# Moving two state products and an add between VectorE, GpSimd and TensorE in a fused scan and expert kernel

## The reference

```python
xn = layernorm(x)                                  # x: 32 sequences x 512 steps x 256 channels
# state space part, 16 states n per channel
delta, B, C = split(xn @ W_deltaBC.T, [64, 80])
delta  = softplus(delta @ W_dt.T + b_dt)
deltaA = exp(delta[..., None] * -exp(A_log))
BX     = delta[..., None] * B[:, :, None, :] * xn[..., None]
hs     = scan over the 512 steps: h[t] = deltaA[t] * h[t-1] + BX[t]
y      = einsum('blds,bls->bld', hs, C) + D * xn
# 8 experts, each takes its 128 best rows of every sequence
G, I = top_k(softmax(xn @ Wg), 128)
ffn  = scatter_add(G * (gelu(xn[I] @ W1 + b1) @ W2 + b2), I)
out  = x + y + ffn
```

## Time and profile before

| | |
|---|---|
| median of 3 runs | 2426.65 us (2425.75 to 2430.33) |
| the profiled execution | 2422.32 us, its span 2420.4 us |
| busy share of the span | PE 94%, PEld 75%, DVE 97%, ACT 86%, POOL 89% |
| DVE instructions with C | L1008 x448, mean 1216 ns |
| POOL adds to ysum | L585 x415 and 32 first ones |
| loads of b_wide | x128, 512 KB each, median 4.5 us to landing |

### The profile page before, as it was taken

One profiled execution on the slowest core, in us unless ns is written; L12 is line 12 of the kernel. 1 busy time (PEld: TensorE's weight loads), 2 busy tenths in 40 slices (PEclk: granted clock), 3 DMA queues, 4 the chain that ended last, 5 costly groups with the idle time before them and its releaser, 6 DMA issues. The chain is left out here.

```text
span 2420.4 us, 33772 instructions
## 1 busy us (share of the span) xinstructions
PE 2286.8 (94%) x10756; PEld 1816.4 (75%) x10756; DVE 2349.7 (97%) x1975; ACT 2074.3 (86%) x3629; POOL 2146.5 (89%) x1235
## 2 busy tenths in 40 slices
PE   7749999999999999999999999999999999999996
PEld 4437777777777777777777777777778777777775
DVE  5799999999999999999999999999999999999997
ACT  7748889898888888988888889888898989888884
POOL 5527999999999899999999999999999999999997
PEclk9969999999999999999999999999999999999998
DMA  9967575645656565555656555565646456565444
GB/s 344 338 209 266 158 221 157 177 136 148 168 147 173 145 161 141 165 154 134 184 137 173 136 166 145 141 176 143 177 127 180 127 151 163 149 173 139 128 127 79
DMA packets 151649, 403.04 MB, mean 167 GB/s; under 512 B 19536, under 2 KB 88240, under 8 KB 134832
## 3 DMA queue, kind: packets, MB, share of 16 engines
q1 hardware_dynamic: 84208, 316.72, 38.2%
q0 software_dynamic: 66048, 83.92, 20.6%
q10 hardware_dynamic: 1216, 0.23, 0.0%
HBM read 323.72 MB, written 91.75 MB: 172 GB/s over the span
## 5 line engine op out<-in xcount | busy, mean ns | idle before, releaser
L585 POOL TENSOR_TENSOR ysum<-ysum,prod 128x1024 f32<-128x1024 f32 x415 | 1121.4, 2702 | 20.3 <-DVE prod L1008 12.1
L997 DVE TENSOR_TENSOR_SCAN bank_x<-decay,bank_x 128x1024 f32<-128x1024 f32 x448 | 1024.7, 2287 | 8.9 <-DVE bank_x L936 0.5
L1163 PE MATMUL bank_l<-ext,w_sb 128*128 128x256 f32 x4096 | 968.9, 384 | 28.2 <-ACT og L757 22.6
L1229 PE MATMUL bank_l<-w_sb,hid 128*128 128x256 f32 x4096 | 939.0, 382 | 0.0
L1163 PEld LDWEIGHTS bank_l<-ext,w_sb 128*128 128x128 f32 x4096 | 760.3, 191 | 166.5 <-ACT og L757 31.0
L1229 PEld LDWEIGHTS bank_l<-w_sb,hid 128*128 128x128 f32 x4096 | 767.5, 190 | 130.0 <-issue 29.0
L717 ACT ACTIVATE decay<-delta,a_sb 128x511 f32<-128x511 f32 x1024 | 641.9, 707 | 15.8 <-POOL delta L517 14.6
L936 DVE TENSOR_TENSOR bank_x<-du,bank_b 128x1024 f32<-128x1024 f32 x512 | 617.6, 1206 | 4.7 <-ACT bank_b L748 3.2
L726 ACT ACTIVATE hid<-bank_l,b_all 128x256 f32<-128x256 f32 x1024 | 431.5, 475 | 203.8 <-PE bank_l L1163 200.7
L1008 DVE TENSOR_TENSOR prod<-bank_x,c_all 128x1024 f32<-128x1024 f32 x448 | 544.9, 1216 | 0.1
L540 POOL DMA_INDIRECT out<-og,idx_all x256 | 410.0, 1601 | 43.8 <-POOL ysum L585 42.5
(11 more groups left out here) (117 smaller groups left out, 1958.9 us busy)
## 6 DMA issues: line engine op xcount, KB each, us to landing
c_all<-bc_rows SPq DMA_DIRECT2D x128, 1024.0 KB, 5.1
b_wide<-bc_rows SPq DMA_DIRECT2D x128, 512.0 KB, 4.5
w_sb<-in_w SPq DMA_DIRECT2D x32, 1024.0 KB, 9.3
decay<-in_x SPq DMA_DIRECT2D x32, 512.0 KB, 6.8
xn_rows<-c_all SPq DMA_DIRECT2D x32, 512.0 KB, 6.5
out<-yrow POOLq DMA_DIRECT2D x32, 512.0 KB, 8.5
xr<-xn_rows SPq DMA_DIRECT2D x30, 512.0 KB, 6.0
bc_rows<-prod SPq DMA_DIRECT2D x32, 192.0 KB, 5.1
```

The source lines that it names most:

```text
L585: nc.gpsimd.tensor_tensor(ysum[:, m % 2], first, prod[:, i], ALU.add).then_inc(sum_done, 1)
L997: nc.vector.tensor_tensor_scan(into, decay[:, k % 2, i].rearrange("p c t -> p (c t)"), bank_x[:, s % 2], 0.0, ALU.mult, ALU.add).then_inc( ...
L1163: i = nc.tensor.matmul(bank_l[(q + v) % 2][:, (f % 2) * UT:(f % 2 + 1) * UT], w1_sb[:, e2, hc, f * P:(f + 1) * P], ext[:, v % 2, hc], star ...
L1229: i = nc.tensor.matmul(o, hid[:, w % 2, f, c * K:(c + 1) * K], w2_sb[:, w_par, f], start=False, stop=(f == FC - 1 and c == UB - 1))
```

## The change

States 4, 14 and 15 are now `GP_STEPS`, so POOL makes three products per batch; `KEPT` is (14, 15). The scans of 14 and 15 write to `kept[:, 0]` and `kept[:, 1]`, POOL multiplies in place, and both stay terms of their own, which PE sums. State 8 is now an ordinary state. Of the last batch DVE makes the products 14 and 15 itself. The two gathers of a unit stand behind step 0 and behind step 3 of the quarter. In the first quarter ACT copies the B rows 2 and 3 and PE spreads 0 and 1. The last y is summed term by term, as each term gets ready, into `bank_t` and `bank_l[0]`.

```diff
-GP_STEPS = (4, 8)
-KEPT = 8
+GP_STEPS = (4, 14, 15)
+KEPT = (14, 15)
-WIDE = (1, 2)
+WIDE = ((2, 3), (1, 2), (1, 2), (1, 2))
...
+        def by_gp(s):
+            return s % N in GP_STEPS and not (s // N == NB - 1 and s % N in KEPT)
+        def stays(s):
+            return s % N in KEPT and s // N < NB - 1
...
 # SP, load_b_wide(u)
-                held(b_ready, (u - 1) * STEPS + WIDE[-1] + 1)
+                held(b_ready, (u - 1) * STEPS + WIDE[(u - 1) % SLOTS][-1] + 1)
...
 # POOL
-            def gather(u):
+            def gather(u, i):
...
-                            if n in GP_STEPS:
+                            if by_gp(s):
                                 pool.wait_ge(scan_done, s + 1)
                                 pool.wait_ge(c_in[u % 2], (u // 2 + 1) * 16)
-                                from_, to = (kept[:, m % 2], kept[:, m % 2]) if n == KEPT else (state[:], prod[:, i])
+                                from_, to = (kept[:, n % 2], kept[:, n % 2]) if stays(s) else (state[:], prod[:, i])
...
-                            if n > 0 and n != KEPT and s < NB * N - 1:
+                            if n > 0 and n not in KEPT:
                                 nc.gpsimd.tensor_tensor(ysum[:, m % 2], first, prod[:, i], ALU.add).then_inc(sum_done, 1)
...
-                        if i == 0:
-                            if there(u + 3, NU):
-                                gather(u + 3)
+                        if i in (0, 3) and there(u + 3, NU):
+                            gather(u + 3, i // 3)
...
 # ACT
-                        if there(u, NU) and pair in (0, 2):
-                            spread_b(u * STEPS + WIDE[pair // 2])
+                        if there(u, NU) and pair == 2:
+                            spread_b(u * STEPS + 2)
+                        elif there(u, NU) and pair == 0 and sl > 0:
+                            spread_b(u * STEPS + 1)
...
+                    if there(u, NU) and sl == 0:
+                        spread_b(u * STEPS + 3)
...
 # DVE
-                        if n == KEPT:
-                            wait(dve, y_tr, b * 2 - 2)
-                            into = kept[:, par].rearrange("p c t -> p (c t)")
+                        if stays(s):
+                            wait(dve, y_tr, b * 2)
+                            into = kept[:, n % 2].rearrange("p c t -> p (c t)")
...
-                        if n in GP_STEPS:
+                        if by_gp(s):
                             continue
...
 # PE, y_rows
-                        terms = [ysum[:, par, dt, rows], kept[:, par, dt, rows], skip[:, par, dt, rows]]
+                        terms = (ysum[:, par], kept[:, 0], kept[:, 1], skip[:, par])
...
+            def last_term(term, half, first=False, last=False):
+                into = bank_l[0] if half else bank_t[:]
+                for c in (2 * half, 2 * half + 1):
+                    for dt in range(HC):
+                        o = nc.tensor.matmul(into[:, (c % 2) * D + dt * P:(c % 2) * D + (dt + 1) * P],
+                                             term[:, dt, c * P:(c + 1) * P], ident[:],
+                                             start=(first and c % 2 == 0 and dt == 0), stop=(last and c % 2 == 1 and dt == HC - 1), is_transpose=True)
+                return o
...
-                            if q % 2 == 0 and (n + 1) % STEPS not in WIDE and there(s + 1, NB * N):
+                            if q % 2 == 0 and (n + 1) % STEPS not in WIDE[(n + 1) % N // STEPS] and there(s + 1, NB * N):
...
-                        if q in (5, 6) and u == NU:
+                        if q == 5 and u == NU:
+                            par = (NB - 1) % 2
                             pe.wait_ge(yrow_done, NB * 2 - 2)
...
+                            pe.wait_ge(og_done, NU * UB)
                             pe.wait_ge(skip_done, NB)
-                            y_rows((NB - 1) % 2, q - 5, True)
+                            for half in range(2):
+                                last_term(skip[:, par], half, first=True)
+                            pe.wait_ge(sum_done, sums(NB * N))
+                            for half in range(2):
+                                last_term(ysum[:, par], half)
+                            for n in KEPT:
+                                pe.wait_ge(prod_done, dve_prods((NB - 1) * N + n + 1))
+                                for half in range(2):
+                                    o = last_term(prod[:, n % STEPS], half, last=(n == KEPT[-1]))
+                                    if n == KEPT[-1]:
+                                        o.then_inc(y_tr, 1)
```

More of the change, by code:

```diff
@@ L130, in build @@
         rank = sb("rank", [R, T])
-        b_wide = sb("b_wide", [P, len(WIDE), T])
+        b_wide = sb("b_wide", [P, 2, T])
         bcs = sb("bcs", [3 * 2 * N, 2, T], BF16)
@@ L502, in _ @@
                 pool.wait_ge(rows_out[r], 16 * NB // 4)
-            def gather(u):
+            def gather(u, i):
                 wait(pool, ex_tr, u - 1)
                 pool.wait_ge(picks_done, 2 + u // 64 * 2)
[L508 to L512, removed]
+                pool.indirect_dma_start(
+                    out=ex[:, u % 2, i], out_offset=None, in_=xn_rows,
+                    in_offset=bass.IndirectOffsetOnAxis(ap=idx_all[:, u * UB + i:u * UB + i + 1], axis=0),
+                ).then_inc(gathered[u % 2], 16)
             def take_delta(nb, par):
@@ L525, in _ @@
             for v in range(2):
-                gather(v)
+                for i in range(UB):
+                    gather(v, i)
             take_delta(1, 0)
             take_du(1, 0, 16)
-            gather(2)
+            for i in range(UB):
+                gather(2, i)
             split_rest(NG - 1)
@@ L597, in main @@
                             scatter(u - 1, 1)
-                        if i == 2 and u == NU - 1:
-                            scatter(u, 1)
-                            scatter(u, 0)
+                        if i in (1, 2) and u == NU - 1:
+                            scatter(u, 2 - i)
                         if i == 3 and sl == 0 and there(b - 2, NB) and u < NU:
@@ L747, in spread_b @@
                 act.wait_ge(bx_done, s)
-                nc.scalar.copy(bank_b[:], b_wide[:, s % STEPS - WIDE[0]]).then_inc(b_ready, 1)
+                nc.scalar.copy(bank_b[:], b_wide[:, s % STEPS - WIDE[s // STEPS % SLOTS][0]]).then_inc(b_ready, 1)
             def scale_og(w):
@@ L1097, in y_ready, with y_rows @@
                 pe.wait_ge(skip_done, y + 1)
-            def y_rows(par, half, last=False):
-                into = bank_x[:, 0, 0:T] if last and half else bank_t[:]
+            def y_rows(par, half):
                 for c in (2 * half, 2 * half + 1):
                     for dt in range(HC):
-                        part = into[:, (c % 2) * D + dt * P:(c % 2) * D + (dt + 1) * P]
+                        part = bank_t[:, (c % 2) * D + dt * P:(c % 2) * D + (dt + 1) * P]
                         rows = slice(c * P, (c + 1) * P)
-                        terms = [ysum[:, par, dt, rows], kept[:, par, dt, rows], skip[:, par, dt, rows]]
-                        if last:
-                            terms.append(prod[:, STEPS - 1, dt, rows])
+                        terms = (ysum[:, par], kept[:, 0], kept[:, 1], skip[:, par])
                         for t, term in enumerate(terms):
-                            o = nc.tensor.matmul(part, term, ident[:], start=(t == 0), stop=(t == len(terms) - 1), is_transpose=True)
+                            o = nc.tensor.matmul(part, term[:, dt, rows], ident[:],
+                                                 start=(t == 0), stop=(t == len(terms) - 1), is_transpose=True)
                 o.then_inc(y_tr, 1)
+            def last_term(term, half, first=False, last=False):
[6 more added lines that the diff above has]
+                return o
             def spread_b(s, n, par):
```

23 lines of the change are left out of this document (10 added, 13 removed).

## The result

The changed kernel takes **2725.97 us** (median, 2724.80 to 2728.89) against 2426.20 us of the kernel before (2424.30 to 2430.33) on the same chip: the ratio is 1.1235, with a 95% interval of 1.1215 to 1.1254. The prediction was 2401 us, a little faster; the kernel is 12% slower. The span of the profiled run is 2725.0 us.

A forecast was written before the change was run, and what follows sets the result against it. DVE was taken as the bound, with POOL and the ACT-PE loop within 1.2 us. DVE -26.7, POOL +5 and the end -4.2 make -25.9 us: 2396.4 us profiled, 2401 us as median, range 2389 to 2416 (8 in 10).

The forecast's parts named there:

- the parting of the gathers on POOL: POOL's gathers issued apart: 10.6 us a batch with gaps become 9.5 to 10.0 us.
- SP: Loads of c_all and b_wide go out later but were expected in time; nothing counted.
- DVE: 13 products a batch in place of 14: batch 68.37 us, -26.7 us in all.
- POOL's size: POOL's batch 68.4 to 69.0 us, taken as 68.6, 0.2 above DVE's; cost 5 us, ends 0 and 20.
- Rival 1: POOL at its upper end, or the loop of ACT and PE, decides: batch 69.1 us, 2411 us; chance 0.20.
- The end: Last y summed by terms: 2.1 us from last product in place of 6.3, so -4.2 us.
- PE and ACT: Eight more PE transposes a batch (0.87 us) covered by idle time, ACT's copies as many as before; loop 68.3 us.
- Rival 4: Handing over saves nothing, as bx waits for its B row around bx 15, 0 and 1: 2422 us; chance 0.04.
- rival 3: Late b_wide load holds ACT's copy of row 5 in the second quarter; 2442 us if landing takes 10; chance 0.06.
- The sum: DVE -26.7, POOL +5 and the end -4.2 make -25.9 us, from 2422.3 to 2396.4 us profiled.

The follow-up runs named there:

- e7_again: Changed kernel with gathers parted forward (first behind step 3 of the unit before, second behind step 0), timed once more: 2391.46 us, ratio 0.9871.
- e1_paired: Changed kernel with both gathers of a unit again behind step 0, the rest of the change kept: 2408.71 us, ratio 0.9935.
- e6_second_at2: Changed kernel with the second gather of a unit behind step 2 in place of step 3: 2426.07 us, ratio 1.0017.
- e4_paired_old_wide: Changed kernel with both gathers behind step 0 and ACT copying the old B rows 1 and 2 in the first quarter: 2410.7 us, ratio 0.9941.

## Why the prediction was wrong

**The step that failed** is the parting of the gathers on POOL: "Parted, they are eight of 1.0 with six gaps of 0.15 ... 9.5 to 10.0 us. ... POOL's batch is then 69.4 less 0.4 to 1.0". It was counted as POOL's own time, a gain of up to 1 us a batch. Who reads the second gather, and how long it had been waiting for its reader, was never asked. The same text works out that product 15 ends at about 1231.4 us, and uses that for c_all only. The gather stands behind the same product. Issued at 1231.4 + 0.27 = 1231.7, with the 2.8 us after which rows arrive (median in the trace of the kernel before), PE would have had them at 1234.5 at best. But PE's 16 matmuls of the up part run from 1224.43 for 3.72 us, and the transposes stand right behind them, so they are due at 1228. PE would thus be some 6.3 us late in every batch, which is 195 us if all of it is passed on. The runs show that most of it is: with small loads and a busy PE the late gather costs 74.19 - 69.03 = 5.16 us a batch, 160 us in all, against the pairs. How much of the lateness the circle takes up could not be read from the rows. None of the four rivals had this place: they looked at the engines' sums, at bx's B rows and at the loads of SP.

**What it was worth.** The place alone is about half of the loss. The other half are two effects of the late gather: it falls beside a load of 1 MB, and it lets PE's clock fall. The first was in the text in another form, as "SP ... Nothing counted": c_all was asked whether it comes in time, and it does. What it does to the transfer next to it was left out. The second, the clock, was in no part of the text.

**DVE** was right. It makes 418 products, and its batch was put at 68.37 us; in `e7_again`, where it waits for next to nothing, it is 68.52.

**POOL's size** was right where the gathers don't come late: "68.4 to 69.0; I take 68.6". It is 69.03 with the pairs, and at most 68.52 parted forward, so the gaps that the text counted on are real. Rival 1 (a batch of 69.1 by POOL, 2411 us) is what the change does with paired gathers: 2408.71.

**The end** was right. From the end of the last product to the copy of `yrow` the changed kernel takes 2.0 us (2714.25 to 2716.24), against 2.1 in the prediction. Its transposes of that product are these:

```profile
2714.30 1.11 PE L1127 MATMUL bank_t<-ident,prod 128*128 128x128 f32 x4 [0.24 <-DVE prod L1019]
2715.21 0.99 PE L1127 MATMUL bank_l<-ident,prod 128*128 128x128 f32 x4
```

The same place in `e7_again`:

```profile
2377.86 1.23 DVE L1023 TENSOR_TENSOR prod<-bank_x,c_all 128x1024 f32<-128x1024 f32 x1
2379.14 0.66 PE L1131 MATMUL bank_t<-ident,prod 128*128 128x128 f32 x4 [0.34 <-DVE prod L1023]
2379.63 0.60 PE L1131 MATMUL bank_l<-ident,prod 128*128 128x128 f32 x4
...
2380.27 0.69 DVE L1030 COPY yrow<-bank_l 128x512 f32<-128x512 f32 x1 [1.19 <-PE bank_l L1131]
```

From 2379.09 to 2380.27 are 1.2 us, against 6.3 in the earlier trace rows. Fewer transposes were expected, not faster ones: the second four start 0.49 us after the first four here and 0.91 in the changed kernel, where the earlier trace rows gave 0.228 us for one. That 0.8 us is luck either way, as the last section shows.

**PE and ACT** held as costs. The eight more transposes a batch hid: PE is busy for 2087.69 of the 2100 us of 250:2350 in `e7_again`. The exchanged B rows were put at nothing; that was right as a cost, but the text took them for neutral, and they are needed. Rival 4 named the short steps around bx 0 and 1 as the danger, and without the exchange that danger is real (17.6 us). **b_wide** (rival 3) was late by up to 1.9 us in 16 batches of `e1_paired`, where POOL's 69.03 us hid it, and once in `e7_again`.

The sum, -25.9 us, left the late gather out, so it can be held against the runs in which no gather is late. With the gathers parted forward it holds: 0.9884 and 0.9871 of 2422 us are -28 and -31 us. With pairs, whose gaps it had counted away, it is -15.

## What to carry to other kernels

When a transfer is moved later in a queue, find its reader first: the time from its issue to that reader, less what it takes to land, is the slack, and what is beyond it lengthens the period if the reader's work leads back to the queue, here by 5.2 of some 6.3 us. To have it stand apart from another, move one forward rather than the other back. And a wait that opens inside a closed loop grows by what it falls beside: the loads issued on the same event, and the lower clock of the engine that idles.

## What the hardware showed

- PE had the rows of a gather (128 of 1 KB) 2.82 us after its issue in `e6_second_at2`, and after 5.96 us when 1 MB for c_all went out 0.2 us ahead of it. Making the loads of c_all and b_wide an eighth as large gave 107 us of 2726 back, though nobody had waited for c_all.
- 36 transposes that nobody reads made the kernel 41.7 us faster. They fill a wait of PE that is on the path: eight matmuls behind it take 1.89 instead of 3.62 us.
- The same two levels are in the tail. In the kernel before, PE did nothing for 8.9 us ahead of the last transposes, and they began at a granted clock of 0.50, the 1.2 GHz level. With the terms summed one by one the last eight transposes ran at 1.00 in `e7_again`, but at 0.55 in the changed kernel, from the same order of work ahead of them. Of the twelve profiles with this tail (that of `e4_paired_old_wide` aside) six take 1.2 us from the last product to the copy and six 1.6 to 2.1. So summing by terms takes transposes off the path; what decides the clock of the last ones isn't shown. The stretches, kernel before and `e7_again`:

```profile
2404.00:2408.00 4.00, 2.19 (x11) 2.23 (x12) 1.44 (x2) 0.00 (x0) 3.53 (x3) 0.50 0.30 37
```

```profile
2379.00:2380.30 1.30, 1.09 (x8) 0.86 (x8) 0.11 (x2) 0.47 (x1) 0.00 (x0) 1.00 0.84 94
```
